# A three-block language tower on one core: mixture-of-experts stage with one PSUM bank per tile, four gelu buffers, five copied weights, a second tile list in two parts, a combine in two steps, and new instruction orders

## The reference, cut to what matters

```
x_norm = layernorm(h); probs = softmax(x_norm @ gate_w)         # 8 experts
dispatch_w, expert_idx = top_k(probs, 2)
for e in range(8):
    y = gelu(x_norm @ w1[e] + b1[e]) @ w2[e] + b2[e]            # 128 -> 512 -> 128
    out += combine[:, e] * y
h = h + out
```

## Time and profile before

| what | value |
|---|---|
| median of 3 runs | 455.56 us (452.96 to 459.41) |
| the profiled execution | 456.4 us, its span 454.9 us |
| PE busy in the span | 358.6 us (79%) |
| DVE, ACT, POOL busy | 291.4, 200.6, 148.4 us |
| granted TensorE clock, mean | 0.905 |
| expert products (L1015 and L1026) | from 327.7 to 437.3 us |
| combine and output | from 437.3 us to the end |

### The profile page before, as it was taken

One profiled execution on the slowest core, in us unless ns is written; L12 is line 12 of the kernel. 1 busy time (PEld: TensorE's weight loads), 2 busy tenths in 40 slices (PEclk: granted clock), 3 DMA queues, 4 the chain that ended last, 5 costly groups with the idle time before them and its releaser, 6 DMA issues. The chain is left out here.

```text
span 454.9 us, 8331 instructions
## 1 busy us (share of the span) xinstructions
PE 358.6 (79%) x2525; PEld 270.3 (59%) x2525; DVE 291.4 (64%) x904; ACT 200.6 (44%) x425; POOL 148.4 (33%) x154
## 2 busy tenths in 40 slices
PE   2653777968998999999999784968997397888830
PEld 2322555557466846787558643537997386788720
DVE  1598896598799759996879639864464232222306
ACT  1247473644653857036522144202483343456514
POOL 6764022341402410131031705560016435453530
PEclk9995959988999999999999968796999599889985
DMA  5999900000000000000082100111201222110016
GB/s 157 352 362 374 377 2 0 3 1 0 0 2 1 1 0 3 0 3 0 2 294 77 43 6 13 36 41 38 60 14 36 60 75 71 40 31 22 31 45 238
DMA packets 19667, 33.11 MB, mean 73 GB/s; under 512 B 4746, under 2 KB 13330, under 8 KB 19240
## 3 DMA queue, kind: packets, MB, share of 16 engines
q1 hardware_dynamic: 16584, 26.52, 16.5%
q0 software_dynamic: 3040, 6.06, 4.3%
HBM read 18.78 MB, written 14.24 MB: 73 GB/s over the span
## 5 line engine op out<-in xcount | busy, mean ns | idle before, releaser
L1228 ACT ACTIVATE arena<-bank,arena 128x128 f32<-128x128 f32 x156 | 44.1, 369 | 47.4 <-PE bank L1015 18.2
L1026 PE MATMUL bank<-big,arena 128*128 x312 | 44.0, 290 | 16.8 <-ACT arena L1228 13.1
L1026 PEld LDWEIGHTS bank<-big,arena 128*128 128x128 f32 x312 | 39.5, 200 | 19.8 <-issue 19.7
L721 POOL DMA_INDIRECT dealt<-xy,arena x32 | 32.6, 1019 | 25.5 <-DVE arena L1597 16.8
L1667 DVE COPY w1s<-big 128x512 f32 x39 | 17.7, 453 | 34.8 <-PE bank L1015 24.3
L921 PE MATMUL bank<-xT_f,wq 128*128 128x512 f32 x64 | 31.0, 632 | 0.0
L1504 DVE TENSOR_TENSOR arena<-bank,causal 128x512 f32<-128x512 f32 x32 | 20.4, 682 | 12.9 <-remote 7.2
L711 POOL TENSOR_TENSOR arena<-arena 128x8 f32<-128x8 f32 x4 | 6.6, 1659 | 64.7 <-DVE arena L1518 49.1
L1186 ACT ACTIVATE arena<-bank 128x512 f32<-128x512 f32 x12 | 6.8, 596 | 43.6 <-PE bank L942 24.9
L729 POOL DMA_INDIRECT experts_out<-arena x19 | 18.7, 984 | 19.0 <-DVE arena L1671 14.1
L1015 PE MATMUL bank<-arena,w1s 128*128 128x128 f32 x152 | 20.9, 291 | 2.9 <-issue 2.3
(11 more groups left out here) (277 smaller groups left out, 880.2 us busy)
## 6 DMA issues: line engine op xcount, KB each, us to landing
dealt<-lb SPq DMA_DIRECT2D x9, 924.5 KB, 10.8
big<-in_tv SPq DMA_DIRECT2D x2, 2048.0 KB
big<-in_ew SPq DMA_DIRECT2D x16, 256.0 KB, 6.0
arena<-dealt SPq DMA_DIRECT2D x19, 64.5 KB, 1.8
wq<-in_wq SPq DMA_DIRECT2D x1, 1024.0 KB
vv<-experts_out SPq DMA_DIRECT2D x2, 512.0 KB, 5.0
out<-h SPq DMA_DIRECT2D x4, 256.0 KB, 2.3
b2e<-in_eb SPq DMA_DIRECT2D x1, 512.0 KB
```

The source lines that it names most:

```text
L721: pool.indirect_dma_start(xs, bass.IndirectOffsetOnAxis(ap=goal[b][:, k, t:t + 1], axis=0), xy[b % 2][:, k, t, :], None).then_inc(s_deal[b ...
L1026: last = pe.matmul(p[:, 0:D], hid[n % 2][:, c * P:(c + 1) * P], big[:, bass.ds(e * FF + (E * FF + c * D), D)], start=(c == 0), stop=(c == ...
L1228: last = act.activation(hid[n % 2][:, c * P:(c + 1) * P], of("K.up", n)[:, c * P:(c + 1) * P], ACT.Gelu, bias=eb1[:].rearrange("p e c -> p ...
```

## The change

- `K.down` gets no bank of its own: the down products write into columns 0 to 127 of the tile's up bank (their gelus have been read out by then), and the bank is freed by y (`"K.up": "K.dve2.y"`).
- `DEEP = 4` hid buffers, in the storage of `ht`, in place of two; the gelus of tile n wait for the down products of tile n-4.
- `WAYS = 5` buffers w1s in place of three; the two new ones lie in `lnu` and `kab`.
- Z is cut in three: Z0 makes the first list as before; Z1 counts, after sequence 2, what is left of sequences 0 to 2; Z2 makes the second list of 22 tiles in two parts: first the remainders of sequences 0 to 2 of each expert, then what sequence 3 brought. So tiles 0 to 30 (`EARLY` = 31) hold every row of sequences 0 to 2, and the last eight only rows of sequence 3. Z1 has 6 instructions, Z2 15, with tables of 22x16 in place of 22x8.
- The second list comes in 6 batches in place of 7. `OWN` = 27 tiles are gathered into xg0 in place of 19.
- M of sequences 0 to 2 waits only for the scatters of tiles below 31. M3 (and Y3 and U3) is done in two halves of two token groups each; L1684 is two instructions of half size per sequence. The layout of `experts_out` has the two results of a token side by side.
- All orders are new. In POOL's, W0 and W1 come before R3.3, and behind it comes W11 where there was W3. In all of them the turns of the layers are moved by a few places too.

```
-SPLIT = ((3, 4, 4, 3, 3), (2, 4, 3, 4, 3, 4, 2))
+SPLIT = ((3, 4, 4, 3, 3), (2, 4, 4, 4, 4, 4))
-OWN = 19
-WAYS = 3
+EARLY = 31
+OWN = 27
+WAYS = 5
+DEEP = 4
...
 pool, before:
- ... I2.1 F3.3 R1.3 R2.3 I3.1 R3.3 W3.0 W4.0 W5.0 W7.0 W8.0 W0.0 W1.0 W2.0 W14.0 W15.0 W6.0 W11.0
- W12.0 W13.0 W19.0 W9.0 W10.0 W20.0 W17.0 W16.0 W21.0 W22.0 W18.0 W23.0 W24.0 W25.0 W26.0 W27.0 W28.0 W30.0
- W31.0 W32.0 W29.0 W33.0 W34.0 W35.0 W36.0 W37.0 W38.0
 pool, after:
+ ... I2.1 R1.3 F3.3 R2.3 I3.1 W0.0 W1.0 R3.3 W11.0 W12.0 W7.0 W8.0 W13.0 W14.0 W17.0 W9.0 W3.0 W4.0
+ W5.0 W10.0 W19.0 W20.0 W6.0 W21.0 W22.0 W2.0 W23.0 W24.0 W25.0 W15.0 W16.0 W18.0 W27.0 W28.0 W26.0 W29.0
+ W30.0 ... W38.0
 pe, from the first expert tile, after:
+ ... G14.8 K0.1 G15.8 K1.1 K2.1 K3.1 K0.3 K4.1 K5.1 K1.3 I3.3 K2.3 K3.3 I3.5 Q2.0 K4.3 K5.3 K6.1 Q3.0 R3.1
+ K7.1 K8.1 K6.3 K9.1 K10.1 K7.3 K8.3 K9.3 K11.1 K10.3 K12.1 K11.3 Q4.0 K13.1 K12.3 K14.1 K15.1 K13.3 K14.3
+ K15.3 Q5.0 K16.1 K17.1 K18.1 K16.3 Q6.0 K17.3 K19.1 K20.1 K18.3 Q7.0 K21.1 K19.3 K20.3 K22.1 K23.1 K24.1
+ K25.1 K21.3 Q8.0 K26.1 K22.3 K23.3 ...
 dve, after (a part):
+ ... K4.4 K5.4 R3.0 R3.2 Z2.0 K6.4 K7.4 K11.0 K12.0 K8.4 K9.4 K13.0 K14.0 K15.0 K10.4 K16.0 K11.4 K12.4
+ K17.0 K18.0 K19.0 K20.0 K13.4 K14.4 K15.4 K21.0 K22.0 K23.0 K24.0 K16.4 K17.4 K18.4 K25.0 K26.0 K19.4 ...
...
-                "K.up": "K.act.ht", "K.down": "K.dve2.y"}
+                "K.up": "K.dve2.y"}
-        hid = [take([P, S]) for i in range(2)]
+        hid = [ht[:, i, :] for i in range(DEEP)]
...
             def section_M(b, ph):
                 if b == 0:
                     for q in range(len(BATCHES)):
-                        sp.wait_ge(s_yo[q], 16 * BATCHES[q][2])
+                        if FIRST[BATCHES[q][0]] + BATCHES[q][1] < EARLY:
+                            sp.wait_ge(s_yo[q], 16 * BATCHES[q][2])
...
+                if b == B - 1 and ph == 0:
+                    for q in range(len(BATCHES)):
+                        if FIRST[BATCHES[q][0]] + BATCHES[q][1] >= EARLY:
+                            sp.wait_ge(s_yo[q], 16 * BATCHES[q][2])
+                part = slice(ph * T // 2, (ph + 1) * T // 2) if b == B - 1 else slice(0, T)
+                sp.dma_start(yg[b][:, part].rearrange("p t k c -> p (t k c)"),
+                             yo.rearrange("(b p t k) d -> b p t (k d)", b=B, p=P, k=2)[b][:, part]...)
...
-                    p = room(pe, "K.down", n)
+                    p = of("K.up", n)
...
-                    wait(act, "K.pe2.down", n - 2)
+                    wait(act, "K.pe2.down", n - DEEP)
...
                 for t in range(T):
-                    did(dve.scalar_tensor_tensor(hb[:, t, :], yg[b][:, 0, t, :], wts[:, b * T + t, 0:1], hb[:, t, :],
+                    if t % 2 == 0:
+                        dve.wait_ge(s_yg[b + (t // 2 if b == B - 1 else 0)], 16)
+                    did(dve.scalar_tensor_tensor(hb[:, t, :], yg[b][:, t, 0, :], wts[:, b * T + t, 0:1], hb[:, t, :],
                                                  ALU.mult, ALU.add), "Y.dve.a%d" % t, b)
-                did(dve.tensor_tensor(hb, hb, yg[b][:, 1], ALU.add), "Y.dve.h", b)
+                    if t % 2:
+                        did(dve.tensor_tensor(hb[:, t - 1:t + 1], hb[:, t - 1:t + 1], yg[b][:, t - 1:t + 1, 1], ALU.add),
+                            "Y.dve.h%d" % (t // 2), b)
```

More of the change, by code:

```diff
@@ L587, in section_U @@
             def section_U(b, ph):
-                wait(sp, "Y.dve.h", b)
-                sp.dma_start(out[b * S:(b + 1) * S, :].rearrange("(t p) d -> p t d", p=P),
-                             h[:, b * T:(b + 1) * T, :]).then_inc(s_out, 16)
+                if b < B - 1:
+                    wait(sp, "Y.dve.h1", b)
+                    part = slice(0, T)
+                else:
+                    wait(sp, "Y.dve.h%d" % ph, b)
+                    part = slice(ph * T // 2, (ph + 1) * T // 2)
+                sp.dma_start(out[b * S:(b + 1) * S, :].rearrange("(t p) d -> p t d", p=P)[:, part],
+                             h[:, b * T:(b + 1) * T, :][:, part]).then_inc(s_out, 16)
             each("sp", {"X": section_X, "M": section_M, "V": section_V, "U": section_U})
-            sp.wait_ge(s_out, 16 * B)
+            sp.wait_ge(s_out, 16 * (B + 1))
         @block.gpsimd
@@ L1597, in section_R, with tables @@
                     did(dve.tensor_copy(goal[b][:], spotf[:]), "R.dve.pi", b)
-            def section_Z(f, ph):
+            def tables(z, n, e, cols):
+                into = "Z%d.dve." % z
+                did(dve.tensor_tensor(ej[:, 0:n, 0:e], number[:, 0:n].unsqueeze(2).to_broadcast([P, n, e]),
+                                      cols.unsqueeze(1).to_broadcast([P, n, e]), ALU.is_ge), into + "ej", 0)
+                wait(dve, into + "ej", 0)
+                did(dve.tensor_reduce(ejr[:, 0, 0:n], ej[:, 0:n, 0:e], X, ALU.add), into + "er", 0)
+                wait(dve, into + "er", 0)
@@ new lines, in offsets @@
+            def offsets(z, n, e, first):
+                into = "Z%d.dve." % z
+                did(dve.tensor_tensor(ejn[:, 0:n, 0:e], ej[:, 0:n, 0:e], gap[:, 1, 0:e].unsqueeze(1).to_broadcast([P, n, e]),
+                                      ALU.mult), into + "en", 0)
+                wait(dve, into + "en", 0)
+                did(dve.tensor_reduce(ejr[:, 2, 0:n], ejn[:, 0:n, 0:e], X, ALU.add), into + "eb", 0)
+                wait(dve, into + "eb", 0)
+                did(dve.scalar_tensor_tensor(ejr[:, 3, 0:n], number[:, 0:n], first, ejr[:, 2, 0:n], ALU.add, ALU.add),
+                    into + "eo", 0)
+                wait(dve, into + "eo", 0)
+                did(dve.tensor_scalar(ejr[:, 4, 0:n], ejr[:, 3, 0:n], float(E * CAP // P), float(P), ALU.min, ALU.mult),
+                    into + "ed", 0)
+                wait(dve, into + "ed", 0)
+                did(dve.tensor_copy(off[z // 2][:], ejr[:, 4, 0:n]), into + "oi", 0)
@@ L1600, in section_Z @@
+            def section_Z(z, ph):
+                f = z // 2
                 n = NT[f]
-                last = f == len(PHASES) - 1
-                if f == 0:
-                    dve.memset(done[:], 0.0).then_inc(s_cap, 1)
-                    dve.memset(taken[:], 0.0).then_inc(s_cap, 1)
+                counts = before[:, (B if z == 2 else B - 1) * T, :].unsqueeze(2).to_broadcast([P, E, 2 * E])
+                if z == 0:
+                    dve.memset(taken[:, 0:1], 0.0).then_inc(s_cap, 1)
+                    dve.memset(base[:, 2 * E:], float(2 * E * CAP // P)).then_inc(s_cap, 1)
@@ L1605, in section_Z @@
                     dve.wait_ge(s_cap, 2)
-                else:
-                    wait(dve, "Z.dve.do", f - 1)
-                wait(dve, "R.dve.rk", PHASES[f][0])
-                did(dve.tensor_tensor(over[:], before[:, (PHASES[f][0] + 1) * T, :].unsqueeze(2).to_broadcast([P, E, 2 * E]),
-                                      (full[:, 0:2 * E] if last else full[:, 1:2 * E + 1]).unsqueeze(1).to_broadcast([P, E, 2 * E]),
-                                      ALU.is_gt if last else ALU.is_ge), "Z.dve.gt", f)
@@ L1645, in section_Z @@
-                wait(dve, "Z.dve.ed", f)
-                did(dve.tensor_copy(off[f][:], ejr[:, 4, 0:n]), "Z.dve.oi", f)
-                if not last:
-                    did(dve.tensor_scalar(taken[:, 0, 1:], ntile[:, 2], float(n), None, ALU.min), "Z.dve.ca", f)
-                    wait(dve, "Z.dve.ca", f)
-                    did(dve.tensor_tensor(taken[:, 1, 0:E], taken[:, 0, 1:], taken[:, 0, 0:E], ALU.subtract), "Z.dve.cd", f)
-                    wait(dve, "Z.dve.cd", f)
-                    did(dve.tensor_tensor(done[:], done[:], taken[:, 1, 0:E], ALU.add), "Z.dve.do", f)
+                    wait(dve, "R.dve.rk", B - 2)
@@ new lines, in section_Z @@
+                    wait(dve, "C.pe.kv", B - 1)
+                    did(dve.tensor_tensor(over[:], counts, full[:, 1:2 * E + 1].unsqueeze(1).to_broadcast([P, E, 2 * E]),
+                                          ALU.is_ge), "Z0.dve.gt", 0)
+                    wait(dve, "Z0.dve.gt", 0)
+                    did(dve.tensor_reduce(ntile[:, 0], over[:], X, ALU.add), "Z0.dve.nt", 0)
+                    wait(dve, "Z0.dve.nt", 0)
+                    did(dve.tensor_tensor_scan(ntile[:, 1], ntile[:, 0], ntile[:, 0], 0.0, ALU.add, ALU.bypass), "Z0.dve.in", 0)
@@ new lines, in section_Z @@
+                    wait(dve, "Z0.dve.in", 0)
+                    tables(0, n, E, ntile[:, 1])
+                    did(dve.tensor_scalar(ejr[:, 1, 0:n], ejr[:, 0, 0:n], float(E - 1), None, ALU.min), "Z0.dve.em", 0)
+                    wait(dve, "Z0.dve.em", 0)
+                    did(dve.tensor_copy(eid[0][:], ejr[:, 1, 0:n]), "Z0.dve.ei", 0)
+                    did(dve.tensor_scalar(gap[:, 1, 0:E], ntile[:, 0], -1.0, float(CAP // P), ALU.mult, ALU.add), "Z0.dve.de", 0)
+                    wait(dve, "Z0.dve.de", 0)
@@ L1670, in section_K @@
                     e = expert.pop(n)
```

(3 more changed lines are left out.)

131 lines of the change are left out of this document (75 added, 56 removed), and 90 rows, old and new, of the table ORDER.

## The result

The changed kernel takes **434.05 us** (median of 4 runs, 432.39 to 435.5) against 454.26 for the kernel before in the same rounds (452.12 to 459.41): ratio 0.957, 95% interval [0.951, 0.963], so 20 us less. The forecast of 440 was 6 us too high and its range held.

What follows compares the result with a forecast made beforehand. PE's completion signals were taken to be held during POOL's back-to-back indirect DMAs. From 456.4 us, 6.5 (end), 4 (deals) and 6 (scatter runs) were subtracted, giving 439.9, so 440 us; range 431 to 450.

Steps and rivals of the forecast that it cites:

- What bounds the kernel: Expert stage: PE's completion signals go unseen while POOL issues three or more indirect DMAs back to back; 23.7 us held.
- The formula (count x 1.28 - 3 + 1.6): Held time per POOL run: from about 3 us after its first indirect DMA until 1.6 us after its last.
- The third rival: Expert stage: holds have nothing to do with POOL's runs, so only the end is won: 450 us, chance 0.10.
- The end: Combine after the last product: about 11 us in place of 17.6; gain booked 6.5 us, bounds 4.5 and 7.5.
- The loads of a half: Combine of the last sequence: each half's 256 KB load takes between 2.3 and 3.6 us, taken as 2.9.
- DVE's start at E + 0.5: Combine: DVE starts on three loaded sequences 0.5 us after E, the last product's end.
- The run of deals: Sequence 3's deals: POOL's run is 8 long, ending at 353.4 instead of 357.3; booked 4 us, bounds 1 and 7.
- The runs of scatters: Expert stage behind the deals: deeper buffers, not shorter runs, cover holds; booked 6 us, bounds nothing and 15.
- the bank a tile longer in hand: Expert stage: an up group waits for a bank given back seven tiles earlier, not three and a half; within the 6 us.
- Before 327 us: Layers before the expert stage: only the order moves, direction unknown; booked 0, bounds -4 and +4 us.
- PE-bound to the end: Rival, expert stage: deeper lead covers nearly all 23.7 us, third term 15, time 431 us; chance 0.12.
- DVE's queue: Rival, expert stage: weight copies ahead of ys delay bank release, costing 14.4 us, time 464 us; chance 0.07.

Runs made afterwards that it cites:

- the exchanges: Layer orders before the expert stage, with SP's weight-load order, swapped between kernels: changed kernel with old orders 441.4 us; kernel before with new orders 450.61 us.
- the last pair of experiments: Ten small memsets behind every deal and scatter on POOL: added to the changed kernel, 419.22 us; added to the kernel before, 428.76 us.
- pairs: Changed kernel with POOL waiting after each second indirect DMA, deals and scatters, until it has landed: 450.99 us, ratio 0.989.

## Why the prediction was right, and where it wasn't

**What bounds the kernel: right.** That PE's signals are held while POOL issues indirect DMAs one behind the other was read from one stretch of 12.6 us. Three things now bear it out: almost no run longer than two, and PE's idle time in the expert stage is 6.4 us; memsets that put 0.3 us more between two DMAs, and PE works through a run of eight; a run of 16, and PE gets half as much done. The formula (count x 1.28 - 3 + 1.6) is too strict. One signal came through in the middle of the changed kernel's run of deals, and one did so in the very run it was read from: a copy of DVE, and PE behind it at 351.36, went on some 7 us after the first deal and 7 before the run's end.

```profile
350.53 0.58 DVE L1667 COPY w1s<-big 128x512 f32 x1 [1.75 <-remote]
```

With memsets between the DMAs more come through. What stands between them counts as much as their number. Whether signals of ACT and DVE are held too was not looked into.

The Trainium skill, page "SBUF — State Buffer", section "Who interferes with whom", says that a DMA never contends with a compute engine and that PE and ACT never wait on anyone. For the ports of the SBUF nothing here speaks against it: the products themselves don't become longer (8 of them take 1.06 us at full clock, beside the deals and elsewhere). For what a program sees of PE the runs speak against it: the same instructions with POOL's DMAs 0.3 us further apart, and memsets in between, end 16 us sooner. The third rival, built on that rule, fell.

**The end: right.** Booked 6.5, measured 6.2 in the traces and 6.8 when it is taken away. The tail was put at 11 us and is 11.4. The loads of a half were put at 2.9 us and have a median of 3.0; DVE's start at E + 0.5 was at E + 0.4. The 2.6 us that the prediction worked out from the Trainium skill, page "DMA: Bandwidth & Descriptors", section "Anatomy of one DMA — SWDGE (gpsimd) path", were 0.4 too low; the fit there is for DMAs that POOL issues, and these are SP's.

**The run of deals: right.** Booked 4, measured 4.1, with the resumption 1.7 us behind the eighth DMA.

**The runs of scatters: right in size, half right in cause.** Booked 6, measured 5.5; PE's idle time behind 360 us is 59.4 - 53.75 = 5.7 us, below the 8 that I had named. The size is what is left of the stage when the deals' 4.1 are taken off, not a measurement of its own. The gelu buffers are a part of it (2.4 to 6 us with their orders, not clear of noise); the bank a tile longer in hand, which I had priced in the same sentence, gave nothing measurable. How the rest divides between new orders and five copies was not tested.

**Before 327 us: wrong.** The step was "only the order moves [...] Nothing says which way it goes: 0, bounds -4 and +4". It measured 8.2 us in the traces, some 2 of them chance, and 4 to 7 in the exchanges. The sum came out 6 us too high by this term alone: with it at 7 the forecast would have been 433. Rows to price a part of it were at hand: the same mechanism that I had read at 343 us sits at 296.8, with PE idle for 6.35 us beside POOL's eight deals. I had said that the deals "with their holds" lie there, and then did not ask what PE has in its order during each of them. That PE's new order has more turns there whose inputs are ready before the run is likely, but it was not counted; by the last pair of experiments the holds are some 5.6 of the 8.2 us.

**The rivals.** "PE-bound to the end" had 431, close to the 434 measured, but not for its reason: PE is idle for 13.8 us in the expert stage. DVE's queue did not become the bound: PE's one long wait for a copy (7.8 us) is the hold itself, since the copy waits for PE's held signal.

## What to carry to other kernels

A stall that is understood in one stage is to be looked for over the whole span before a change of order is priced at nothing: here a fifth to a third of the gain lay where the forecast had looked away. Where an engine stops for signals that another engine's instructions hold back, take away the cause before building cover for it: the cover of the change bought 11 us, ten memsets between POOL's DMAs, 0.3 us more of distance, bought 16 on top of it and 27 without it. And a brake is to be priced as a rate: waiting for every second landing freed PE for 14 us and cost 28 in POOL's own queue.

## What the runs showed of the hardware that was not expected

- With POOL's indirect DMAs 1.27 us apart (0.96 to 0.98 us each, 0.30 idle), completions of PE's products reach DVE up to 8 us late in the last run of 8 deals (ended at 341.0, y at 349.24), and PE is stopped for 7.85 us. With four memsets between them (1.43 us apart) it is 4.7 late and a stop of 4.04, with ten (1.57) 2.7 late and a stop of 1.04. What in the chip holds the signals was not found, nor whether time or the memsets let them through.
- Small memsets between two indirect DMAs partly hide in the idle time that is there anyway: ten of them, 0.45 us busy, move the next DMA by 0.30 us.
- With a wait for the landing POOL is idle for 1.6 us behind a deal and 2.1 behind a scatter before the next DMA, in place of 0.30.
- The granted clock follows the holds: 0.91 in the expert stage before, 0.93 after, 0.96 with ten memsets, 0.99 with pairs, where PE is idle for 22.6, 13.8, 9.4 and 6.4 us.
